# Decoder of twelve sublayers on one core: dense layer half by half with GpSimd's scaling behind the splits, and two VectorE moves in the one-bit mixture and the last attention

## The reference, cut to what matters

```python
# layer 1, first sublayer ends in a dense feed-forward; then cross attention
h = _layernorm(src, ln1_g, ln1_b)
h = h + relu(h @ W1 + b1) @ W2 + b2
return _layernorm(h, ln2_g, ln2_b)
...
x = x + _L1_xattn_ref(ctx_2048, _layernorm(x, axis=-1), mask_BxS2_ik0, L1_xattn_b)
...
# layer 2, feed-forward: one shared expert and one of eight, weights of one bit and a sign
shared_out = jax.nn.silu(jnp.einsum('btd,fd->btf', h, sw1)) @ sw2.T
probs = jax.nn.softmax(h @ router_w.T, axis=-1)
...
gate = jax.nn.one_hot(top_idx, N_EXPERTS, dtype=h.dtype) * top_prob[..., None]
return shared_out + routed_out
...
x = x + _L3_attn_ref(_layernorm(x, axis=-1), L3_attn_w_qkv, L3_attn_w_out)
```

## Time and profile before

| what | value |
|---|---|
| median of 3 runs | 1093.16 us (1091.53 to 1093.32) |
| the profiled execution, its time | 1096.35 us |
| its span in the profile | 1094.6 us |
| PE busy | 955.7 us (87%) |
| DVE busy | 628.3 us (57%) |
| ACT busy | 489.4 us (45%) |
| POOL busy | 347.2 us (32%) |
| chain that ended last | PE 66%, DVE 24%, POOL 3%, issue 3%, ACT 2% |
| mean granted TensorE clock | 0.936 of full speed |

### The profile page before, as it was taken

How to read it: one execution, slowest core, us unless ns; L and a number is a source line. 1 busy time by engine, 2 the same in 40 slices (tenths; PEclk the granted TensorE clock), 3 DMA queues, 4 the chain that set the end, 5 groups by cost and what they waited for, 6 DMA issues and landing times.

```text
span 1094.6 us, 16931 instructions
## 1 busy us (share of the span) xinstructions
PE 955.7 (87%) x6484; PEld 703.4 (64%) x6484; DVE 628.3 (57%) x1268; ACT 489.4 (45%) x1115; POOL 347.2 (32%) x443
## 2 busy tenths in 40 slices
PE   5997899989769899999577777999996978869998
PEld 3555789965556588984122225777765965649897
DVE  5575942268855752230899996545575357852322
ACT  1573334347424463344565452434344437715332
POOL 6850289545246200010166562211220016310000
PEclk9698799989988899999699899899999998979999
DMA  5700011000010001103000001000000000000111
GB/s 121 236 1 10 1 40 39 30 20 1 2 38 2 11 20 40 39 11 115 0 1 0 1 0 39 1 1 1 1 1 1 1 1 1 1 10 14 45 40 29
DMA packets 32266, 26.50 MB, mean 24 GB/s; under 512 B 3574, under 2 KB 28346, under 8 KB 31803
## 3 DMA queue, kind: packets, MB, share of 16 engines
q1 hardware_dynamic: 32187, 25.43, 7.7%
HBM read 24.89 MB, written 0.52 MB: 23 GB/s over the span
## 4 chain that ended last, share of the span: by engine, by line
PE 66%; DVE 24%; POOL 3%; issue 3%; ACT 2%; SPq 0%; DMA 0%; DVEq 0%; POOLq 0%; ACTq 0%
PE banks L839 19%; PE banks L821 14%; DVE work L1393 7%; PE banks L342 4%; PE banks L333 4%; DVE banks L1387 4%; PE banks L1558 3%; PE banks L1566 3%; PE banks L365 2%; DVE work L489 2%; PE banks L1580 1%; PE banks L1617 1%; PE banks L1605 1%; DVE keep L129 1%; PE banks L1186 1%
## 5 line engine op out<-in xcount | busy, mean ns | idle before, releaser
L881 ACT ACTIVATE work<-banks,keep 128x512 f32<-128x512 f32 x236 | 157.1, 688 | 191.6 <-PE banks L821 191.4
L839 PEld LDWEIGHTS banks<-keep,work 128*128 128x128 f32 x1888 | 223.4, 194 | 11.0 <-DVE keep L950 5.7
L839 PE MATMUL banks<-keep,work 128*128 128x128 f32 x1888 | 224.6, 277 | 5.3 <-DVE keep L950 5.2
L821 PE MATMUL banks<-rounded 128*128 128x512 f32 x672 | 181.3, 419 | 13.9 <-DVE rounded L930 11.2
L955 DVE SCALAR_TENSOR_TENSOR keep<-banks,keep 128x128 f32<-128x128 f32 x256 | 72.1, 344 | 206.1 <-PE banks L839 205.9
L821 PEld LDWEIGHTS banks<-rounded 128*128 128x128 f32 x672 | 128.5, 200 | 43.9 <-DVE rounded L930 13.0
L657 ACT ACTIVATE work<-banks,work 128x128 f32<-128x128 f32 (+1 forms) x448 | 121.6, 388 | 39.7 <-DVE work L481 32.0
L143 POOL TENSOR_TENSOR keep<-keep 128x4 f32<-128x4 f32 x26 | 26.8, 1030 | 294.7 <-DVE keep L122 241.8
L1431 POOL TENSOR_TENSOR work<-work,keep 128x1024 f32<-128x1024 f32 x32 | 75.3, 2354 | 92.1 <-DVE work L1393 92.1
L481 DVE TENSOR_REDUCE work<-banks 128x8 f32<-128x1024 f32 (+1 forms) x64 | 69.1, 1080 | 52.3 <-PE banks L333 52.2
L1393 DVE TENSOR_TENSOR_SCAN work<-work,banks 128x1024 f32<-128x1024 f32 x32 | 73.2, 2286 | 1.1
(11 more groups left out here) (270 smaller groups left out, 1366.7 us busy)
## 6 DMA issues: line engine op xcount, KB each, us to landing
keep<-in_L_ffn_w_dram SPq DMA_DIRECT2D x32, 256.0 KB, 3.0
keep<-in_L_ffn_W_dram SPq DMA_DIRECT2D x16, 256.0 KB, 3.0
keep<-in_L_xattn_Wkv_dram SPq DMA_DIRECT2D x1, 2048.0 KB, 8.4
keep<-in_L_ffn_expert_w_dram SPq DMA_DIRECT2D x8, 128.0 KB, 2.4
keep<-in_L_ffn_expert_w_dram SPq DMA_DIRECT2D x1, 1024.0 KB, 7.5
keep<-in_halves_dram SPq DMA_DIRECT2D x1, 1024.0 KB, 9.6
keep<-in_L_attn_conv_w_dram SPq DMA_DIRECT2D x1, 1024.0 KB, 8.8
keep<-in_ctx_dram SPq DMA_DIRECT2D x1, 960.0 KB, 8.0
```

Source lines behind the costliest of these rows:

```text
L821: m = pe.matmul(k.ps[:, c, :], w[:, c * P:(c + 1) * P], x[:, h * HALF:(h + 1) * HALF], start=j == 0, stop=j == len(parts) - 1)
L839: m = pe.matmul(k.ps[:, 4 + n % 2, j * P:(j + 1) * P], k.hT[n % 2][:, c, j * P:(j + 1) * P], w2[c], start=c == 0, stop=c == self.nf - 1)
L881: act.activation(k.hT[n % 2][:, c, :], k.ps[:, c, :], self.func, bias=bias, scale=scale)\
```

## The change

Four edits. In `Experts.tensor`, the dense layer alone does `layer2(n)` ahead of `layer1(n + 1)`. On GpSimd, `DenseStart.pool_half(0)` waits until both halves of the dense layer's input are split. In `dense_sums`, for the second half, `n6.normal(0)` stands ahead of `centre`. In the one-bit mixture, `add(0)` stands at the end of the split, ahead of `route`. In the last stretch of the mixture, `l3_attn.first_parts` stands ahead of the statistics of half 1.

```diff
@@ Experts.tensor
+            if self.kind == "dense":
+                self.layer2(pe, n)
             if n + 1 < self.items:
                 self.layer1(pe, n + 1)
             elif tail is not None:
                 tail(pe)
-            self.layer2(pe, n)
+            if self.kind != "dense":
+                self.layer2(pe, n)
@@ Experts.vector_start
         self.split_x(dve, 1)
+        if self.kind == "bit":
+            self.add(dve, 0, self.k.x)
         if self.routed:
             self.route(dve)
@@ Experts.vector
-    def vector(self, dve, after=None, done=None):
+    def vector(self, dve, after=None, done=None, last=None):
...
         for n in range(self.items):
-            self.add(dve, n, k.x)
+            if n or self.kind != "bit":
+                self.add(dve, n, k.x)
...
                 dve.wait_ge(*self.acc_done.upto(n + 1))
+                if h and last is not None:
+                    last(dve)
                 token_stats(k, dve, k.x, range(4 * h, 4 * h + 4))
@@ dense_sums
                 l1_after.variance(dve, h)
+                if h:
+                    n6.normal(dve, 0)
                 l1_after.centre(dve, h)
                 if h:
-                    n6.normal(dve, 0)
                     l1_cross.first_parts(dve)
                 l1_after.add(dve, h, n6)
@@ VectorE's queue
-            l2_ffn.vector(dve, n12, done=lambda dve, n: l3_attn.first_parts(dve) if n == l2_ffn.items - 1 else None)
+            l2_ffn.vector(dve, n12, last=l3_attn.first_parts)
@@ GpSimd's queue
             l1_attn.pool(pool, n4)
+            pool.wait_ge(*l1_dense.x_split.upto(2))
             for h in range(2):
                 l1_start.pool_half(pool, h)
```

## The result

| what | before | changed |
|---|---|---|
| median of all runs taken together | 1094.19 us (13 runs, 1091.53 to 1098.09) | 1087.56 us (13 runs, 1084.02 to 1090.84) |
| ratio | | 0.9933 (0.992 to 0.9946) |
| the profiled execution, its span | 1096.35 us, 1094.6 us | 1087.56 us, 1085.8 us |
| mean granted clock | 0.936 | 0.941 |

By the ratio the change saves 7.3 us (5.9 to 8.8); the medians are 6.6 us apart. The forecast was 3.5 us. The sign was right and the size was not. The median of 1087.56 us lies just inside the forecast range (1087.3 to 1092.5), but by luck: the kernel before measured 1094.19 us in 13 runs and not the 1093.16 us of three runs from which the forecast started.

What follows compares the result with a forecast made beforehand. The dense layer was taken as bound by the split, then TensorE, then VectorE's queue. Dense layer -3.8, mixture -1.1 and last attention +1.4 made -3.5 us, from 1093.16 to 1089.7 us, range 1087.3 to 1092.5.

Steps and rivals of the forecast that it cites:

- the last attention's: Last attention: GpSimd's power waits for the variance, now behind the blocks, so the scores come later: +1.4 us (+0.9 to +1.9).
- All behind it moves too, and TensorE ... with it: Last attention: everything behind GpSimd's power, released at 902.95 instead of 901.55, and TensorE shift by the full +1.4 us.
- The dense layer's -3.8: Dense layer: cross attention's first blocks start at 321.2 against 325.01, -3.8 us (bounds -4.3 and -1.4).
- The mixture's -1.1: One-bit mixture: `layer2(3)` ends at 852.9 against 854.0, -1.1 us (bounds -2.0 and +0.7).
- GpSimd ... 11.73 us plus gaps of 0.1: Dense layer: GpSimd's six scalings, bias and power take 11.73 us plus gaps from 302.35, so the power is ready at 314.2.
- I let the shift pass through whole: Between dense layer and mixture: one queue with weights loaded long ahead, so the whole -3.8 us carries through.
- in the middle of `layer2(3)`: One-bit mixture: the slow clock ends near 852, partway through `layer2(3)`, which so takes 2.7 us.
- the slow time lasted 3.8 us: One-bit mixture: slow clock of 3.8 us read from the old trace, counted anew from 848.4 to near 852.
- The rule that I weighed: Dense layer: `centre`'s four instructions each stand still beside one of GpSimd's, power included; `AfterNorm.add` 0.5 us later, sum -3.0.
- GpSimd's queue is the bound: Rival: dense layer -1.4 or somewhat better, mixture 0, attention +1.4; total -0.3 to -1.5 us, chance 0.22.
- A dense layer at slow clock: Rival: TensorE runs slow in the dense layer from 300.4; +2.8, with the attention +4.2 us, 1097.4 us, chance 0.04.
- the mixture keeps its clock: Rival: `layer2(3)` in the mixture is fast and the last attention's statistics cost nothing; -5.5 us, 1087.7 us, chance 0.10.

Runs made afterwards that it cites:

- the filling: 16 more matmuls of 512 columns, read by nothing, in TensorE's mixture gap behind `layer2(2)`, added to the whole change: 1083.01 us, ratio 0.9897 against the kernel before.

## Why the prediction had the sign right and the size wrong

The sum missed by 3.8 us. Of the terms, the last attention's was furthest off (+1.4 forecast, -0.6 measured): the step that failed there is "All behind it moves too, and TensorE ... with it". The dense layer's -3.8 was -5.3 (-5.0 with all profiles): GpSimd's chain was put 0.5 us too long, and the clock that the old gap cost in some executions was not in the sum. The mixture's -1.1 was -0.5 and made up for a part.

- **Direction and steps: right.** The split is no longer held back, `layer2(0)` starts on ScalarE's end, `AfterNorm.add` of half 0 waits for GpSimd's power, `centre` fills the gap ahead of the blocks, the scores wait 1.36 us longer. The rows that the prediction named look as it said, but for the second product of item 3 in the mixture.
- **Dense layer, -3.8 forecast, -5.3 measured.** The step that failed is "GpSimd ... 11.73 us plus gaps of 0.1" by its size, and the premise that the old trace's clock stands for the kernel. GpSimd's chain took 11.37 us (303.62 to 314.99), since the three scalings of each half took 3.97 and 3.98 us and nothing stretched them; that is 0.5 us gained beyond the forecast, and with `layer1(0)` slow, as in the old trace, the path is in fact 4.35 shorter. The other 1 us of the four-profile mean (0.7 with all six and seven profiles) is the clock: in two of the six executions `layer1(1)` behind the old gap took a further 1.2 us, which the change saves by having no gap. I had read 0.95 for the clock in the gap and priced only the idle time.
- **What moved the most: attributed wrongly.** The working hung the gain on GpSimd's wait and costed TensorE's order behind it only. Without the wait the order gives 4.4 us of path and 0.9945, against 0.9939 for all three. That a sum built on the wait came as near to the dense layer's gain as it did is luck in part: the order gives as much by another way.
- **"I let the shift pass through whole": failed, in my favour.** From the blocks to the split at 405 the changed kernel is another 0.9 us shorter in the mean of four. With the two further profiles of the old dense layer (79.44 and 79.49 us) and the three of the changed one (79.92, 79.93 and 79.97) the means are 79.8 and 79.5, so a gain here is not shown. What moves it is the slow clock that begins near 320: 10.2 us of it in the first profile of the changed kernel, 17.1 in the second, and 2.55 us between the two in this stretch. (In the two kernels with TensorE's order and without GpSimd's wait it lasted 6.8 us, and the stretch took 77.06 and 77.10 us: 2.4 us less than in most others, beside their gain on the path.) The first and the second profile:

```profile
320.40:330.60 10.20, 7.51 (x28) 5.02 (x27) 8.59 (x31) 1.72 (x5) 4.50 (x11) 0.50 0.01 2
```
```profile
319.90:337.00 17.10, 13.43 (x48) 9.07 (x48) 10.90 (x40) 4.43 (x14) 8.07 (x18) 0.50 0.01 1
```

- **Mixture, -1.1 forecast, -0.5 in the four profiles, 0.9998 alone.** The slow clock was forecast to end "in the middle of `layer2(3)`"; in most executions it lasted through it (3.62 us for 2.7), and in some it ended early. The step behind this is a reading of the earlier trace rows: "the slow time lasted 3.8 us" is the length of the window. The granted clock of 0.71 in the 5.20 us before it says that some 3.0 us of the gap were slow too, 6.8 us in all, and it was 6.8 us again. Its mean over seven profiles is -0.8 us (56.86 against 57.68), all of it from the three short ones, and the ratio alone (-1.7 to +1.3 us) allows it.
- **Last attention, +1.4 forecast: right at the scores, wrong for the whole.** TensorE runs slow there. In the changed kernel the matmuls that follow the scores meet a clock that is up again: L300 and L304 take 1.39 and 1.05 us, where they took 1.91 and 1.45 in the old trace. So a part of a delay just ahead of matmuls that would have run slow comes back behind it: 25 us behind the keys' copy it is 0.5 us, and with the attention's edit alone 0.6. From the keys' copy on, the changed kernel is nevertheless 0.6 us shorter and not 1.4 longer. That comes from one place, 64 to 71 us behind the keys' copy, where all four profiles of the changed kernel turn 0.8 us of delay into 0.9 us of lead. Four matmuls there ran at slow clock in every profile of the kernel before (3.02 to 3.35 us) and at full clock in all four of the changed one:

```profile
964.34 3.35 PE L1045 MATMUL banks<-keep 128*128 128x512 f32 x4
956.72 1.88 PE L1054 MATMUL banks<-keep 128*128 128x512 f32 x4
```

  The attention's edit does not do that by itself: with it alone they took 2.79 us, with the filling added to the whole change 2.91, and from the keys' copy to the end those profiles are 0.2 and 1.0 us longer than the kernel before. Why the slow stretch misses them in the changed kernel stays open.
- **The sum.** All six rows of the table add up to -6.9 us, the difference of the mean spans. Without the +1.3 at the start and the -0.9 in the middle (one profile's stretch at 684), which are of single executions, the others, -5.3, -0.9, -0.5 and -0.6, are -7.3 us. That this is the measured difference to the tenth is chance, given how the rows scatter. Only the path and the end differ by more than they scatter, and the end's -0.6 is not an effect of the attention's edit alone.
- **The rule that I weighed.** `centre`, with two SBUF inputs, did stand still beside GpSimd's wide instructions (4.24 us against 1.14 free). The Trainium skill names VectorE instructions with two SBUF inputs as contending with GpSimd for SBUF in the GPSIMD Engine Reference, under Specifications, and the trace agrees. It cost nothing, since the last of the four ran beside the power of 128x4 in 338 ns and was done 0.65 us before the power. The -3.0 that I worked out by the rule, with the power holding it too, did not come.
- **The rivals.** GpSimd's queue is the bound, but at a price nearer to the good end. A dense layer at slow clock was seen in the kernel before, not in the changed one. That the mixture keeps its clock came in part: in some executions it falls for 3.4 us only. From the 1093.16 that the forecast started from, -7.3 is 1085.9 us, below the range's 1087.3. What the range lacked was the slow clock behind the old gap in some executions, and an attention term that could be negative.

## What to carry to other kernels

Here an idle gap of TensorE cost its length and, in some executions, more slow clock behind it (the path behind it took 28.3 to 28.4 us and not 27.0 in two profiles of six). Count both, and take the second from more than one profile, since one execution shows one way in which it can fall. When an edit of several parts works, run each part alone before saying which did it: here the one that removed the gap was enough, and the one that removed the cause of the gap added nothing until its own price, the bias in GpSimd's queue, was moved away. And cut two traces at the same instructions into five or six stretches, over several profiles of each, and take in every experiment's profile whose code is the same there: four profiles of each kernel put the dense layer at -5.3 us and the next stretch at -0.9, six and more at -5.0 and -0.3.

## What was not expected of the hardware

- Where the slow stretches fall, and for how long, varies between executions of one program. The mixture's, with the change, lasted 3.4 or 6.8 us; the one that begins near 320, 10.2 or 17.1 us; the kernel before reached VectorE's scaling of the dense layer after 293.7 to 299.9 us. The Trainium skill says in "TensorE: Matmul & The Clock Gate", Part 1, that the number of slow matmuls of one kernel changes from run to run; the profiles here agree: the four of the kernel before are up to 6.2 us apart (spans of 1089.8 to 1096.0 us), with 136 to 147 us of slow clock in each.
- 16 useless matmuls (3.94 us) in a gap of 4.4 us gained 2.35 us behind it.
- Contention between VectorE and GpSimd was one-sided: VectorE's four small instructions went from 1.14 to 4.24 us, GpSimd's of 1.27 us stayed at 1.26 to 1.33. Only beside the split's subtraction, a single wide one, did they stretch (1.36 and 1.61 us in the kernel with TensorE's order alone, 1.36 and 1.60 in the kernel before).
